# Pooling two rows of keys to a matmul in a one-core attention-pooling kernel

## The reference

```python
# q (2048, 128), k (2048, 200, 128), mask (2048, 200); H = 64
qe = jnp.broadcast_to(q[:, None, :], k.shape)
feat = jnp.concatenate([qe, k, qe - k, qe * k], axis=-1)
h = feat @ W1 + b1
h = jnp.where(h >= 0, h, alpha[0] * h)
a = (h @ W2 + b2)[..., 0]
a = jnp.where(mask == 0, jnp.float32(NEG), a)
w = jax.nn.softmax(a, axis=-1)
return jnp.einsum('bl,bld->bd', w, k)
```

## Time and profile before

| | before |
|---|---|
| Time, median of 3 runs | 918.41 us (917.94 to 921.9) |
| Profiled execution, its own time | 906.77 us |
| Its span, first to last instruction | 905.1 us |
| PE busy | 801.2 us, 89% of the span |
| DVE busy | 751.3 us, 83% |
| POOL busy | 658.3 us, 73% |
| ACT busy | 446.2 us, 49% |
| DMA queue of the data | 218.93 MB, 74.3% of the 16 engines' span |

### The profile page before, as it was taken

How to read it: one execution, slowest core, us unless ns; L and a number is a source line. 1 busy time by engine, 2 the same in 40 slices (tenths; PEclk the granted TensorE clock), 3 DMA queues, 4 the chain that set the end, 5 groups by cost and what they waited for, 6 DMA issues and landing times.

```text
span 905.1 us, 55310 instructions
## 1 busy us (share of the span) xinstructions
PE 801.2 (89%) x25216; PEld 592.5 (65%) x25216; DVE 751.3 (83%) x887; ACT 446.2 (49%) x1281; POOL 658.3 (73%) x401
## 2 busy tenths in 40 slices
PE   1779989988999999898999988899999899899995
PEld 0547766666667667666667766666776667676674
DVE  4889888887888889788988888889998789898870
ACT  0345545545555555444555544455555455554551
POOL 2668877758777777776778877777887767887761
PEclk9799999999999999999999999999999999999999
DMA  8866888776788788767888886888888588887820
GB/s 238 328 246 198 263 269 259 252 242 227 245 278 260 254 257 292 227 194 252 260 264 278 278 261 194 264 265 279 284 271 288 175 269 277 269 294 246 262 60 12
DMA packets 85449, 222.46 MB, mean 246 GB/s; under 512 B 27360, under 2 KB 35552, under 8 KB 85216
## 3 DMA queue, kind: packets, MB, share of 16 engines
q1 hardware_dynamic: 85216, 218.93, 74.3%
HBM read 214.57 MB, written 4.33 MB: 242 GB/s over the span
## 4 chain that ended last, share of the span: by engine, by line
PE 76%; issue 10%; DVE 10%; ACT 3%; DMA 1%; SPq 1%; POOL 0%; POOLq 0%; DVEq 0%; ACTq 0%
PE hP L175 43%; PE poolP L175 22%; PE scoreP L175 11%; DVE keysT L530 6%; ACT act L472 3%; DVE act L538 3%; DMA keys<-in_r_q 1%; DVE logits L545 1%; DVE keysT L583 0%; SPq L321 0%; SPq L318 0%; SPq L319 0%; POOL pool_w L454 0%; DVE neg_max L551 0%; DVE biast L586 0%
## 5 line engine op out<-in xcount | busy, mean ns | idle before, releaser
L472 ACT ACTIVATE act<-hP,biast 128x200 f32<-128x200 f32 x1024 | 371.7, 425 | 289.6 <-PE hP L175 288.7
L175 PE MATMUL hP<-keysT,weff 32*64 32x200 f32 x16384 | 453.5, 339 | 57.1 <-issue 35.9
L530 DVE STREAM_TRANSPOSE keysT<-keys 128x1536 f32<-128x1536 f32 (+1 forms) x256 | 469.0, 1832 | 0.0
L175 PEld LDWEIGHTS hP<-keysT,weff 32*64 32x64 f32 x16384 | 329.3, 132 | 146.7 <-issue 99.1
L538 DVE TENSOR_TENSOR act<-hP,act 128x400 f32<-128x400 f32 x512 | 282.9, 562 | 116.7 <-ACT act L472 102.8
L415 POOL TENSOR_TENSOR weff<-qX,wp 128x1024 f32<-128x1024 f32 x128 | 243.8, 1905 | 107.0 <-PE hP L175 91.3
L419 POOL TENSOR_TENSOR weff<-weff,wk 128x1024 f32<-128x1024 f32 x128 | 305.5, 2387 | 10.0
L175 PE MATMUL poolP<-keys,pool_w 128*16 128x128 f32 x6400 | 239.1, 273 | 17.1 <-issue 15.8
L175 PEld LDWEIGHTS poolP<-keys,pool_w 128*16 128x16 f32 x6400 | 194.9, 97 | 46.1 <-issue 20.7
L454 POOL TENSOR_TENSOR pool_w<-probs_k,own_b 128x400 f32<-128x400 f32 x128 | 111.5, 872 | 119.0 <-DMA probs_k<-probs_scratch 109.7
L175 PE MATMUL scoreP<-act,w2win 128*16 128x200 f32 x2048 | 140.0, 342 | 4.5 <-DVE act L538 4.0
(11 more groups left out here) (35 smaller groups left out, 29.6 us busy)
## 6 DMA issues: line engine op xcount, KB each, us to landing
keys<-in_r_k SPq DMA_DIRECT2D x256, 576.0 KB, 5.2
keys<-in_r_k SPq DMA_DIRECT2D x128, 448.0 KB, 5.1
probs_scratch<-expd SPq DMA_DIRECT2D x32, 100.0 KB, 3.8
masks<-in_r_mask SPq DMA_DIRECT2D x128, 12.5 KB
probs_k<-probs_scratch SPq DMA_DIRECT2D x128, 12.5 KB
out_rows<-pooled SPq DMA_DIRECT2D x128, 8.0 KB
keys<-in_r_q SPq DMA_DIRECT2D x4, 256.0 KB, 5.1
act<-in_L_rec_W SPq DMA_DIRECT2D x4, 128.0 KB, 6.4
```

Source lines behind the costliest of these rows:

```text
L175: return t_.matmul(*args, **flags)
L472: a_.activation(act[:, h % ABUF, a, :], hP[:, 2 * (p % HSETS) + a % 2, 0:L], ACT.Identity, bias=biast[:, n, k, a:a + 1], scale=slope).then ...
L530: v_.transpose(keysT[:, n % TBUF, j0 * D:j1 * D], keys[:, n % SLOTS, j0 * D:j1 * D]).then_inc(keysT_done, 1)
```

## The change

`pool_keys` takes two rows of keys to a matmul: the weights of rows j and j+1 side by side (128x32) by the keys of both rows (128x256). Of the four blocks of the result the two on the diagonal are wanted. A tile has 12 such matmuls and one single one, for row 24. The strips now hold 32 rows by 256 columns, `parts` holds [P, GT, 256], and `add_parts` takes the wanted blocks out with two matmuls for each tile, one with the first 16 rows of each strip against columns 0 to 127, one with the other 16 against columns 128 to 255: 8 matmuls to a group, not 4. `place` becomes a window that slides over a wider array, one for each half. `HEAD_J` goes from 12 to 16, `STEP_LEN` from 392 to 344, an early load's `free_at` from m + LAG + 0.5 to m + LAG + 0.52. `masks` and `pooled` have one buffer instead of two; the masks of group g+1 are loaded once the scores of group g are read, those of group 1 no longer at the start.

```diff
-HEAD_J = 12
+ROWS = 2
+HEAD_J = 16
-STEP_LEN = 392
+STEP_LEN = 344
...
-        parts = sb("parts", [P, GT, D])
-        pooled = sb("pooled", [P, 2, D])
+        parts = sb("parts", [P, GT, ROWS * D])
+        pooled = sb("pooled", [P, D])
...
-                for j in range(j0, j1):
-                    c = j % QUADS
-                    mm = matmul(poolP[QP * c:QP * c + SUB, 0:D], pool_w[:, m % 2, j, :],
-                                   keys[:, m % SLOTS, j * D:(j + 1) * D], start=(j < QUADS), stop=(j + QUADS >= J))
+                for j in range(j0, j1, ROWS):
+
+                    c, end = j // ROWS % QUADS, min(j + ROWS, J)
+                    mm = matmul(poolP[QP * c:QP * c + SUB * (end - j), 0:D * (end - j)],
+                                   pool_w[:, m % 2, j:end, :].rearrange("p j b -> p (j b)"),
+                                   keys[:, m % SLOTS, j * D:end * D],
+                                   start=(j < ROWS * QUADS), stop=(j + ROWS * QUADS >= J))
...
-                wait(consts_done, GT)
+                wait(consts_done, ROWS)
                 wait(parts_done, GT * (g + 1))
                 for t in range(GT):
-                    mm = matmul(poolP[:, D:2 * D], place[:, t, :], parts[:, t, :], start=(t == 0),
-                                   stop=(t == GT - 1))
+                    x = BQ * (GT - 1 - t)
+                    for h in range(ROWS):
+                        mm = matmul(poolP[:, ROWS * D:(ROWS + 1) * D], place[:, h, x:x + P],
+                                       parts[:, t, h * D:(h + 1) * D], start=(t == 0 and h == 0),
+                                       stop=(t == GT - 1 and h == ROWS - 1))
...
-                    free_at = m + LAG + 0.5 if early else m + LAG + 0.96
+                    free_at = m + LAG + 0.52 if early else m + LAG + 0.96
...
-                    if mask_at[g] == b and g + 2 < GROUPS:
+                    if mask_at[g] == b and g + 1 < GROUPS:
                         sp.wait_ge(scores_read, g + 1)
-                        load_mask(g + 2)
+                        load_mask(g + 1)
...
-                    a_.activation(parts[:, m % GT, :], poolP[:, 0:D], ACT.Copy).then_inc(parts_done, 1)
+                    a_.activation(parts[:, m % GT, :], poolP[:, 0:ROWS * D], ACT.Copy).then_inc(parts_done, 1)
```

More of the change, by code:

```diff
@@ L76, in attention_pooling @@
         act = sb("act", [P, ABUF, QUADS, L])
-        masks = sb("masks", [P, 2, L], I32)
+        masks = sb("masks", [P, L], I32)
         logits = sb("logits", [P, L])
@@ L88, in attention_pooling @@
         own_b = sb("own_b", [P, SUB])
-        quad_b = sb("quad_b", [P, SUB])
-        place = sb("place", [P, GT, P])
+        quad_b = sb("quad_b", [P, ROWS, SUB])
+        place = sb("place", [P, ROWS, BQ * (GT - 1) + P])
         neg = sb("neg", [P, 1])
@@ L311, in load_mask @@
                 for c in range(QUADS):
-                    sp.dma_start(masks[QP * c:QP * c + HALF_Q, g % 2, :],
+                    sp.dma_start(masks[QP * c:QP * c + HALF_Q, :],
                                  mask_rows[g, c]).then_inc(mask_in[g % 2], 16)
@@ L333, in _ @@
                     load_mask(0)
-                    load_mask(1)
                 if n == SLOTS - 1:
@@ L357, in write_out @@
                 for c in range(QUADS):
-                    sp.dma_start(out_rows[g, c], pooled[QP * c:QP * c + HALF_Q, g % 2, :]
+                    sp.dma_start(out_rows[g, c], pooled[QP * c:QP * c + HALF_Q, :]
                                  ).then_inc(out_done[g % 2], 16)
@@ L434, in _ @@
                              pattern=[[KP, SUB]], channel_multiplier=-1).then_inc(consts_base, 1)
[L435 to L444, removed]
+            for h in range(ROWS):
+                for c in range(QUADS):
+                    pool.wait_ge(consts_base, 5 + QUADS * h + c)
+                    g_.affine_select(out=quad_b[:, h, :], in_=quad_b[:, h, :], compare_op=ALU.not_equal, fill=1.0,
+                                     base=-QP * c - SUB * h, pattern=[[-1, SUB]], channel_multiplier=1
+                                     ).then_inc(consts_base, 1)
+            pool.wait_ge(consts_base, 5 + QUADS * ROWS)
+            for h in range(ROWS):
+                g_.tensor_copy(place[:, h, BQ * (GT - 1):].rearrange("p (c z) -> p c z", c=QUADS)[:, :, 0:BQ],
+                               quad_b[:, h, :].rearrange("p (c w) -> p c w", c=QUADS)).then_inc(consts_done, 1)
             for n in range(STEPS):
@@ L500, in _ @@
                     act_e.wait_ge(inv_done, g + 1)
-                    ge(act_e, out_done[g % 2], g // 2 * 16 * QUADS)
-                    a_.activation(pooled[:, g % 2, :], poolP[:, D:2 * D], ACT.Copy,
+                    ge(act_e, out_done[(g + 1) % 2], (g + 1) // 2 * 16 * QUADS)
+                    a_.activation(pooled[:], poolP[:, ROWS * D:(ROWS + 1) * D], ACT.Copy,
                                   scale=inv_sum[:, g % 2:g % 2 + 1]).then_inc(pooled_moved, 1)
@@ L545, in mask_scores @@
                 v_.copy_predicated(logits[:].rearrange("p (i j) -> p i j", i=KP),
-                                   masks[:, g % 2, :].rearrange("p (i j) -> p i j", i=KP),
+                                   masks[:].rearrange("p (i j) -> p i j", i=KP),
                                    scoreP[:, 0:L].rearrange("p (j i) -> p i j", i=KP)
@@ L551, in mask_scores @@
                 v_.tensor_reduce(neg_max[:], logits[:], AX_X, ALU.max, negate=True).then_inc(max_done, 1)
-            v_.memset(masks[:].rearrange("p a l -> p (a l)"), 0).then_inc(zeroed, 1)
+            v_.memset(masks[:], 0).then_inc(zeroed, 1)
             v_.memset(scoreP[:], 0.0)
```

## The result

The changed kernel takes 936.73 us in the median (931.64 to 942.23, 4 runs), the kernel before 920.15 us (917.94 to 936.74, 4 runs), 17 us less. The ratio, which is taken from the undisturbed executions alone, is 1.0264, with a 95% interval from 1.0191 to 1.0336: by it the change costs about 24 us (18 to 31), where the prediction had 9 us. The profiled execution has a span of 940.5 us against 905.1 us.

The account below looks back on a forecast made before the run. PE, busy for 89% of the span, was taken as the bound, losing time to waits for weights and the instruction stream. -2 + 12 + 2 - 15 + 12 = +9 us gave 927 us, range 900 to 953 us.

Parts of the forecast that it names:

- The pooling itself, -2 us: PE's pooling matmuls: streaming columns sets the pace, so halving the count saves only 2 us, bounds -74 and 0.
- The rival of a price to each matmul: PE's pooling: each matmul has its own price, saving 74 us in place of 2, giving 855 us; chance 3%.
- `add_parts`, +12 us: Late step on PE: eight more matmuls a group make 28 us, of which the wait for weights covers 16 us.
- The +2 us for probabilities that come back later: Read-back of probabilities, at most one block later: blocks are longer now, costing 2 us.
- Fewer instructions, -15 us: PE's instruction stream: 176 blocks instead of 198 shorten stalls, 24 us gained, part given back; bounds -46 and +5.
- When the keys come, +12 us: Key loads on SP: issued later, so DVE and then PE wait; 18 us, a third covered; bounds 0 and 60.
- some 20 to 50 us: Sign in the next profile: DVE's idle time before transpositions, ending with a DMA of `keys`, where it had 0.0.
- The estimate of 5.7 us to land: Key landing with SP's wait before issue added: 48 tiles late by 46 us, leaving PE with 30 us.
- the median's row: Key landing of 5.1 us: 33 of 118 tiles late by 24 us together, leaving PE with 12 us.
- a third of it as covered: Late keys: 6 us of PE's 18 us fall where it would wait for weights or instructions anyway.
- The prediction's +9 us: Whole kernel: the sum of all terms, added to the median of the runs, giving 927 us.
- The rival "the keys are in time": Key loads: late keys cost PE under about 4 us, the fetch saves its full 24 us; about 906 us; chance 26%.

Follow-up runs that it names:

- experiment 5: `add_parts` without its matmuls for the second row of each pair: on the changed kernel 920.12 us, on the changed kernel with keys in four parts 916.04 us.
- experiment 3: The kernel before with a third key part to a block allowed earlier (`> 0`), so 65 blocks carry three parts: 978.19 us, ratio 1.0678.
- experiment 4: A tile's keys loaded in four parts instead of three: on the changed kernel 923.05 us, ratio 1.0055; on the kernel before 939.99 us, ratio 1.0227.

## Why the prediction came out as it did

- **The pooling itself, -2 us: right.** Where nothing is waited for, head, rest and late pooling take 0.98, 0.74 and 1.61 us. Six rounds of 128 columns became three of 256 at twice the time. A weight load of 32 columns takes 110 ns and is hidden. The rival of a price to each matmul, and the 60 cycles of overhead of the Trainium skill ("TensorEngine Tiling (Array Packing)", Instruction Overhead), taken as a price on top of each matmul's columns, are not seen here: PE's matmuls fell by 2,816, and those of the pooling have 238.6 us of busy time, where they had 239.1 us.
- **`add_parts`, +12 us: right in kind, too small.** The 28.6 us in all are there. Of the 16 us taken as covered by the wait for weights, 11 were by the profiles, which leaves 17 us; the runs of experiment 5 say 17 us by the medians and 25 us by the ratios. The +2 us for probabilities that come back later was not measured by itself.
- **Fewer instructions, -15 us: the size fits, the reason is narrower.** The stalls of the stream fell from 46 to 30 us from start to start. The prediction had 24 us gained by longer blocks and a part given back to whole tiles in one block; that part was held at a few us. Whole tiles in one block do cost that way: their packets start 1.4 us later (experiment 3). Experiments 3 and 4 show how many key parts a block issues as the stronger lever: it moved the stalls between 46 and 100 us at the same number of instructions. How much of the 16 us is the block's length and how much the filling of the blocks was not separated.
- **When the keys come, +12 us: right in mechanism and too small.** DVE's idle time before transpositions is 62.5 us where "some 20 to 50 us" stood, and PE waits 26 us for activations, 22 us more than before, where 12 were taken. Beside the 17 to 25 us of `add_parts` it is one of two large losses and not the one that decides. The landing got longer, 5.5 us in the median against 5.1: the second and third part of a whole tile in one block take 6.2 and 6.1 us, the second of two parts 5.9 us, where it took 5.5 us; and an output or a mask load stands between the key parts on SP. The estimate of 5.7 us to land, whose 30 us were put aside in favour of the median's row, was nearer. Taking a third of it as covered moved the term away from the 22 us.
- **What the sum left out.** After longer stops of PE its clock was lower. The granted clock of the profiled execution is 0.973 on average against 0.988, so PE was at the lower level, 1.2 GHz, for some 51 us in place of 22. The nine such stretches between 100 and 850 us came each within 2 us of a stop of PE of 2.3 to 3.4 us. At half the clock a stretch loses half of its length, so at most half of the 29 us more, some 14 us, is lost.
- **The sum.** By the profiles: -2 + 28.6 for all of `add_parts` - 4 for the wait for weights (26 to 22) - 16 + 22 = +29 us, and up to 14 us for the clock, for the 35 us between the two profiled executions. With the 17 us of experiment 5 in place of the 28.6 - 4 it is +21 us; the ratio says 24 us (18 to 31). That the two agree so well is partly luck, since the terms come from one execution of each kernel. The prediction's +9 us had the sign and the causes, but less than half of the size: both losing terms were taken too small.
- **The rival "the keys are in time"** was not the case, but experiment 4's edit made its condition true, and the time was 923 us, not 906. The rival had 24 us saved on the stalls, of which 16 were, and had 16 us of the wait for weights used up by `add_parts`; that wait is 32 us there, more than the 26 of the kernel before.

The Trainium skill's sentence that crossing an instruction block is "mostly hidden" ("Runtime: NRT & Kernel Launch", Instruction fetch mechanics) holds in no run here: the stalls that end behind an instruction packet are 13 us at the least (with half of `add_parts`) and 100 us at the most.

## What to carry to other kernels

Where matmuls on different strips of the array run side by side, look at the rounds in the timeline before merging them: if a round takes what its columns take to stream, halving their number gains nothing, and anything added to undo the merge is a loss. In a kernel whose loads are paced by another engine's instruction count, a change to that count changes the plan of the loads; work the lead of each load out again, and the evenness of what each trigger issues, before looking at anything else. A longer stage in one place can make a reordering worthwhile that wasn't before: try the neighbours of the wait that is left.

## What was not expected of the hardware

The instruction stream reacts very strongly to bursts of data. 65 blocks with 1.6 MB in place of 1.1 MB, the total unchanged, made the kernel 62 us slower by the ratio (978 against 920 us by the medians). The granted clock of its profiled execution was this, where the kernel before had 0.988:

```profile
core 0: 980.9 us, clock 0.962
```

Smaller transfers are not gentler by themselves: four parts in place of three cost the kernel before 2.3% (1.6 to 2.9).
